# A two-layer network on one core: expert tiles split into gate, up and down parts, softplus placed earlier, a table of its own for the gather

## The reference, cut to what matters

```
x  = x + L0_attn(layernorm(x)) + L0_ffn(layernorm(x))
x  = x + L1_attn(layernorm(x)) + L1_ffn(layernorm(x))
```

## Time and profile before

| | |
|---|---|
| profiled execution | 2730.79 us |
| its span (first to last instruction) | 2729.0 us |
| median of three runs | 2729.32 us |
| busy: PE, DVE, ACT, POOL | 2148.3, 1660.9, 1149.4, 935.1 us |
| mean granted TensorE clock | 0.874 of full |
| DMA | 175.06 MB, mean 64 GB/s |

### The profile page before, as it was taken

One profiled execution on the slowest core, in us unless ns is written; L12 is line 12 of the kernel. 1 busy time (PEld: TensorE's weight loads), 2 busy tenths in 40 slices (PEclk: granted clock), 3 DMA queues, 4 the chain that ended last, 5 costly groups with the idle time before them and its releaser, 6 DMA issues.

```text
span 2729.0 us, 38765 instructions
## 1 busy us (share of the span) xinstructions
PE 2148.3 (79%) x11640; PEld 1493.1 (55%) x11640; DVE 1660.9 (61%) x2929; ACT 1149.4 (42%) x2667; POOL 935.1 (34%) x581
## 2 busy tenths in 40 slices
PE   3257788887888788887788787887788878888985
PEld 1033456565665556555566555665566555565664
DVE  2954876458754786447765577656774478654432
ACT  2212464235633465234552355424563346523641
POOL 0320482017610384005630077202751048401601
PEclk9568789888899898987898898998889989899997
DMA  2000012211212111220112211221122211132223
GB/s 94 0 16 1 26 52 80 76 68 41 80 58 101 45 48 60 82 97 34 58 56 91 76 41 54 89 88 49 47 70 71 98 41 46 64 119 70 72 93 115
DMA packets 82452, 175.06 MB, mean 64 GB/s; under 512 B 11448, under 2 KB 42560, under 8 KB 81984
## 3 DMA queue, kind: packets, MB, share of 16 engines
q1 hardware_dynamic: 78144, 164.05, 17.7%
q0 software_dynamic: 4096, 8.40, 1.0%
HBM read 123.71 MB, written 15.14 MB: 51 GB/s over the span
## 4 chain that ended last, share of the span: by engine, by line
PE 46%; DVE 16%; issue 15%; POOL 13%; ACT 6%; DMA 3%; SPq 1%; POOLq 0%; DVEq 0%; ACTq 0%
PE G L921 9%; PE G L1043 5%; POOL Y L1935 4%; PE G L1028 3%; DVE HS L1521 3%; POOL REG L1946 3%; POOL REG L1949 2%; POOL YG L1960 2%; PE FM L733 2%; PE G L1060 2%; PE G L932 2%; PE FM L1017 2%; PE FM L891 2%; PE FC L1005 2%; DVE SL L1686 1%
## 5 line engine op out<-in xcount | busy, mean ns | idle before, releaser
L1043 PEld LDWEIGHTS G<-REG 128*128 128x128 f32 x2560 | 361.9, 205 | 64.9 <-issue 51.0
L1521 DVE TENSOR_TENSOR_SCAN HS<-DA,D 128x1024 f32<-128x1024 f32 x128 | 362.7, 2833 | 20.2 <-ACT DA L1204 19.6
L1043 PE MATMUL G<-REG 128*128 128x64 f32 x2560 | 368.9, 278 | 3.2 <-DVE REG L1825 3.2
L1935 POOL TENSOR_TENSOR Y<-Y,HC 128x1024 f32<-128x1024 f32 x114 | 278.4, 2442 | 214.4 <-DVE HC L1543 214.0
L1028 PE MATMUL G<-ident,REG 128*128 128x128 f32 x1280 | 248.8, 295 | 121.2 <-ACT REG L1324 119.2
L921 PEld LDWEIGHTS G<-XGT,MW 128*128 128x128 f32 x1920 | 290.0, 235 | 53.9 <-issue 53.9
L921 PE MATMUL G<-XGT,MW 128*128 128x128 f32 x1920 | 297.4, 321 | 19.0 <-DMA MW<-moe 19.0
L1324 ACT ACTIVATE REG<-G 128x128 f32<-128x128 f32 (+3 forms) x512 | 223.0, 435 | 158.3 <-PE G L1028 154.1
L1946 POOL TENSOR_TENSOR REG<-REG,cos_t 128x512 f32<-128x512 f32 x128 | 178.4, 1394 | 297.0 <-ACT REG L1300 292.1
L1028 PEld LDWEIGHTS G<-ident,REG 128*128 128x128 f32 x1280 | 154.7, 154 | 168.4 <-issue 145.7
L1273 ACT ACTIVATE SL<-G 128x512 f32<-128x512 f32 x120 | 71.6, 597 | 411.5 <-PE G L921 411.5
(11 more groups left out here) (285 smaller groups left out, 3921.2 us busy)
## 6 DMA issues: line engine op xcount, KB each, us to landing
MW<-moe SPq DMA_DIRECT2D x120, 768.0 KB, 4.2
REG<-ROT SPq DMA_DIRECT2D x256, 128.0 KB
EW<-experts SPq DMA_DIRECT2D x16, 514.5 KB, 4.0
XG<-x_rows SPq DMA_DIRECT2D x8, 960.0 KB, 5.5
y_rows<-YO SPq DMA_DIRECT2D x120, 64.0 KB, 1.5
X<-xT SPq DMA_DIRECT2D x8, 256.0 KB, 5.9
W<-weights SPq DMA_DIRECT2D x1, 2048.0 KB, 9.5
REG<-xT SPq DMA_DIRECT2D x8, 256.0 KB, 2.7
```

The costliest lines, as they stand in the source:

```text
L1043: mm = pe.matmul(G[3][:, col:col + DK], PT[:, n % 2, c * P:(c + 1) * P], V[:, c, j * P + h * DK:j * P + (h + 1) * DK], start=c == 0, stop= ...
L1521: dve.tensor_tensor_scan(HS[:, :, :].rearrange("p h s -> p (h s)"), DA[:, n % 2, :, :].rearrange("p h s -> p (h s)"), D1[:, :, :].rearrang ...
L1935: pool.tensor_tensor(Y[:, :, :], Y[:, :, :], HC_EARLY if early else HC[:, n % 2, :, :], ALU.add).then_inc(y_add.sem, 1)
```

## The change

- A tile's `token_use` becomes three parts. `gate` is its four gate products with a semaphore of their own (`gg_mm`), `up` the four up products, `down` the down product. PARTS_AFTER deals the 45 parts over the steps, no more than two after any step; the last, the down product of tile 14, follows step 28 within the list. ACT runs the Tanh with the gate part, waiting for `gg_mm`; DVE runs both products with the up part.
- Softplus (pieces 11 and 12 of the front) moves from after steps 21 and 22 to after steps 17 and 18.
- The gather reads a table of its own, `place_kept`, written from the same places at step 19 of phase 2. The cast into `place_i` at step 9 no longer waits for the picks' sum.

```diff
-        X_AFTER = {0: (1,), 1: (2,), 2: (3,), 3: (4,), 4: (5, 6), 6: (7,), 7: (8,), 10: (9,), 11: (10,), 21: (11,), 22: (12,)}
-        weight = [0.5 if 18 <= p <= 21 else 1.1 for p in range(F_STEPS)]
-        def t_share(p):
-            return 1 + round(sum(weight[:p]) / sum(weight) * (MOE_TILES - 1))
+        X_AFTER = {0: (1,), 1: (2,), 2: (3,), 3: (4,), 4: (5, 6), 6: (7,), 7: (8,), 10: (9,), 11: (10,), 17: (11,), 18: (12,)}
+        TOKEN_PARTS = [("gate", 0), ("up", 0)]
+        for i_ in range(1, MOE_TILES):
+            TOKEN_PARTS += [("gate", i_), ("up", i_), ("down", i_ - 1)]
+        TOKEN_PARTS.append(("down", MOE_TILES - 1))
+        PARTS_AFTER = (0,1,2,1,2,1,2,1,2,1,2,1,2,2,2,1,2,1,2,1,1,1,1,2,2,1,2,1,2,1)
...
-        PHASE_1 = [("o", 0), ("x", 0), ("t", 0), ("f", -1)]
+        PHASE_1 = [("o", 0), ("x", 0), ("t", TOKEN_PARTS[0]), ("t", TOKEN_PARTS[1]), ("f", -1)]
+        PHASE_1 += [("t", u) for u in TOKEN_PARTS[2:2 + PARTS_AFTER[0]]]
+        part_ = 2 + PARTS_AFTER[0]
         for p in range(F_STEPS):
             PHASE_1.append(("f", p))
-            PHASE_1 += [("t", u) for u in range(t_share(p), t_share(p + 1))]
+            PHASE_1 += [("t", u) for u in TOKEN_PARTS[part_:part_ + PARTS_AFTER[p + 1]]]
+            part_ += PARTS_AFTER[p + 1]
...
 (PE)
-            def up_gate(b, i):
+            def gate_rows(b, i):
                 if i >= 2:
                     pe.wait_ge(hh_d.sem, hh_d.at(b, i - 1))
                 pe.wait_ge(xt_copy.sem, xt_copy.at(b, i // TILES + 1))
                 pe.wait_ge(mw_in[i % SLOTS].sem, mw_in[i % SLOTS].at(b, i // SLOTS + 1))
-                g = 2 * (i % 2)
-                for half in range(2):
-                    for c in range(CHUNKS):
-                        at = half * HID + c * P
-                        mm = pe.matmul(G[g + half][:, c * P:(c + 1) * P], MW[:, i % SLOTS, at:at + P], XGT[:, i, :], start=True, stop=True)
+                for c in range(CHUNKS):
+                    mm = pe.matmul(G[2 * (i % 2)][:, c * P:(c + 1) * P], MW[:, i % SLOTS, c * P:(c + 1) * P], XGT[:, i, :], start=True, stop=True)
+                mm.then_inc(gg_mm.sem, 1)
+            def up(b, i):
+                for c in range(CHUNKS):
+                    at = HID + c * P
+                    mm = pe.matmul(G[2 * (i % 2) + 1][:, c * P:(c + 1) * P], MW[:, i % SLOTS, at:at + P], XGT[:, i, :], start=True, stop=True)
                 mm.then_inc(ug_mm.sem, 1)
...
 (ACT)
-                act.wait_ge(ug_mm.sem, ug_mm.at(b, i + 1))
+                if part == "down":
+                    rows_done(b, i)
+                if part != "gate":
+                    return
+                act.wait_ge(gg_mm.sem, gg_mm.at(b, i + 1))
...
 (DVE)
+                if part != "up":
+                    return
...
+                dve.wait_ge(ug_mm.sem, ug_mm.at(b, i + 1))
                 dve.wait_ge(sx_d.sem, sx_d.at(b, i + 1))
...
             def number_places(b):
-                dve.wait_ge(ys_d.sem, ys_d.at(b - 1))
                 dve.wait_ge(xg_in.sem, xg_in.at(b - 1))
                 dve.wait_ge(place_d.sem, place_d.at(b, 11))
                 dve.tensor_copy(place_i[:, :, :].rearrange("p k t -> p (k t)"), places[:, 56:64]).then_inc(place_d.sem, 1)
+            def keep_places(b):
+                dve.wait_ge(ys_d.sem, ys_d.at(b - 1))
+                dve.tensor_copy(place_kept[:, :, :].rearrange("p k t -> p (k t)"), places[:, 56:64]).then_inc(kept_d.sem, 1)
...
+                    if s == KEEP_AT:
+                        keep_places(b)
...
 (POOL, gather)
-                    pool.wait_ge(place_d.sem, place_d.at(t))
+                    pool.wait_ge(kept_d.sem, kept_d.at(t))
...
-                                        in_offset=bass.IndirectOffsetOnAxis(ap=place_i[:, k, c:c + 1], axis=0)).then_inc(yg_in.sem, 16)
+                                        in_offset=bass.IndirectOffsetOnAxis(ap=place_kept[:, k, c:c + 1], axis=0)).then_inc(yg_in.sem, 16)
```

More of the change, by code:

```diff
@@ L162, in build @@
         place_i = sb("place_i", [P, PICKS, TILES], U32)
+        place_kept = sb("place_kept", [P, PICKS, TILES], U32)
         tile_i = sb("tile_i", [1, 16], I32)
@@ L340, in build @@
         place_d = signal("place_d", 12)
+        kept_d = signal("kept_d")
         xw_d = signal("xw_d", PICKS)
@@ L348, in build @@
         xt_mm, xt_copy = signal("xt_mm", TURNS), signal("xt_copy", TURNS)
+        gg_mm = signal("gg_mm", MOE_TILES)
         ug_mm = signal("ug_mm", MOE_TILES)
@@ L376, in build @@
                  d1_mm, d2_mm, lg_mm, wb_mm, e1_mm, e2_mm, v_mm, pj_mm, sc_mm, pt_mm, pv_mm, ot_mm, wo_mm, gl_mm,
-                 xtok_mm, rank_mm, xt_mm, ug_mm, dn_mm, yt_mm] + [n.by_pe for n in norms]
+                 xtok_mm, rank_mm, xt_mm, gg_mm, ug_mm, dn_mm, yt_mm] + [n.by_pe for n in norms]
         by_act = [biased, u_silu, r_silu, soft, da_exp, qsq_d, ksq_d, q_gelu, g_act, d1_gelu, rt_act,
@@ L381, in build @@
                   gk_d, lni_d, hsm_d, m1_d, h2_d, m2_d, l0a_d, xm_d, rt_d, wb_d, yf_d, l0f_d, x2_d, xn2_d, rot_d,
-                  nm_d, rec_d, o_d, x3_d, gt_d, pick_d, place_d, sx_d, hh_d, out_d] + [n.by_dve for n in norms]
+                  nm_d, rec_d, o_d, x3_d, gt_d, pick_d, place_d, kept_d, sx_d, hh_d, out_d] + [n.by_dve for n in norms]
         by_pool = [du_d, skip_y, y_add, y_gate, xnb_d, rope_d, xw_d, ys_d]
@@ L902, in turn_rows, with token_use @@
                 mm.then_inc(xt_mm.sem, 1)
[L904 to L908, removed]
-            def up_gate(b, i):
+            def token_use(b, part, i, following):
+                if part == "gate":
+                    gate_rows(b, i)
+                elif part == "up":
+                    up(b, i)
+                else:
+                    down(b, i)
+            def gate_rows(b, i):
                 if i >= 2:
@@ L1077, in phase_1 @@
                 each_step(b, t, f, filter_step, token_use, front_start, attention_end, early_scan)
-                if t is not None:
-                    down(t, MOE_TILES - 1)
             def phase_2(b, f, t):
@@ L1266, in rows_done, with token_use @@
                 act.activation(YO[:, i % SLOTS, :], G[4][:, 0:D], ACT.Copy).then_inc(yo_copy.sem, 1)
-            def token_use(b, i, following):
-                act.wait_ge(ug_mm.sem, ug_mm.at(b, i + 1))
+            def token_use(b, part, i, following):
+                if part == "down":
[3 more added lines that the diff above has]
+                act.wait_ge(gg_mm.sem, gg_mm.at(b, i + 1))
                 if i >= 2:
@@ L1341, in phase_1 @@
                 each_step(b, t, f, filter_step, token_use, front_start, lambda t, b: None, early_scan)
-                if t is not None:
-                    rows_done(t, MOE_TILES - 1)
             def phase_2(b, f, t):
```

7 lines of the change are left out of this document (3 added, 4 removed).

## The result

The changed kernel took 2618.7 us (median of four runs, 2604.7 to 2623.97), the kernel before 2729.26 beside it: a ratio of 0.958, 95% interval 0.951 to 0.965. The forecast was 2638, its range 2590 to 2692. The profiled execution took 2623.97 us with a span of 2622.1, against 2729.0 before: 106.9 us less.

A forecast was written before the change was run, and what follows sets the result against it. PE is the busiest engine of both phases, yet idle about 26 us of each first phase. Terms 30 + 1 + 54 + 5 + 0 + 1 = 91 us off 2730.8 give 2639.8, as median 2638 us; range 2590 to 2692.

The forecast's parts named there:

- Thirds, idle time: First phase: tiles in thirds fill PE's gaps, idle time from 25.8 to 18.1 us, 7.7 less per lap.
- Clock: First phase: with a third less PE idle time, 0.01 of granted clock comes back, 1.2 us per lap.
- clock comes back: Rival: PE granted 0.95 instead of 0.87 to 0.91 in first phases, about 15 us per lap, time 2598; chance 0.17.
- Own table: Second phase: DVE's cast no longer waits for POOL, 5 us per lap in six laps, 30 us; bounds 2.7 and 6.6.
- the shift at XN2: End of first phase: second phase's first matmul starts about 0.9 us after XN2 instead of 6.57; part of the 7.7.
- Softplus: First phase: 2.4 us gone after the gelus, some 3 of ACT's 7.2 left among them; net 0, bounds -3 and +3 per lap.
- Lap without front and last stage: Outside the six full laps: 5 us without a following front, 1 for the last lap's wait, 1 in the last stage.
- Signs of failure that were named: First phase: PE idle time stays at 26 us, DVE waits for the up third, or a tile's weights come late.
- latency: Rival: the first phase is a chain through PE, ACT and DVE; thirds give 2 us per lap, time 2685; chance 0.18.
- tables: Rival: ACT's 7.2 us of table loads and passes among the gelus uncovered, 23 us slower, time 2752; chance 0.03.

The follow-up runs named there:

- f1: The changed kernel once more, unaltered, on a second chip: 2592.0 us, ratio 0.947 to the kernel before.
- e2: The kernel before with the tiles in thirds alone, no own table, softplus after steps 21 and 22: 2656.2 us, ratio 0.974.
- e4: The changed kernel with softplus back after steps 21 and 22: 2603.3 us, ratio 0.951 to the kernel before.
- e1: The kernel before with the gather's own table alone: 2685.8 us, ratio 0.985.
- g3: The changed kernel with gate, up and down parts put behind one another at one step, signals kept: 2679.3 us, ratio 0.978 to the kernel before.
- h1: The changed kernel with parts dealt finely up to step 18 and put together from there: 2601.3 us, ratio 0.952 to the kernel before.
- e3: The kernel before with softplus alone moved to after steps 17 and 18: 2714.6 us, ratio 0.994.

## Why the prediction was right, and where it was not

- **Total and sign**: 91 us forecast, 106.9 measured between the two profiled executions. This is the sum of first phases that gave 41 us more than their term, second phases that gave 30 less, and 5 more in the rest. That the total came out this near is luck in part, for the two errors have opposite signs. And the 15.9 us a lap of the first phase lie above the 12 with which the range's lower end was added up, though the prediction's own bound was 17.
- **Thirds, idle time**: 7.7 a lap forecast, 10.4 measured (26.0 to 15.6). The closed gaps are among those named: root chain, squares (2.3 left before the variance, where the prediction wanted none), and XN2, which was 0.71 for a forecast 0.9.
- **Clock**: the mis-sized term. 1.2 us a lap was assumed, one hundredth of clock; the mean clock rose by four, from 0.88 to 0.92, and the busy time of the same matmuls fell by 5.4. The price of a hundredth was right, its number not. In the first phase the rival "clock comes back" was nearer than the forecast: it wanted 0.95 and 15 us, and the phase reached 15.9 at about 0.92, as idle time fell more too. f1, at 0.92 to 0.97, shows that both happen.
- **Own table**: that the wait and its 2.12 us cast would go was right; the copy cost 2.6 us in five laps of eight and 0.16 in three, 1.7 on the mean for a forecast 1.1. The term of 5 a lap was too small: 7.7 alone and 6.0 beside the thirds. The stretch from one reciprocal to the next did fall to the 21 us that the prediction named, 21.0 on the mean, but that agreement is luck: it is 19.1 or 19.2 in four laps and 24.0 and 25.8 in two, f1 has 25.3, and alone the table gave 1.2 us there.
- **The step that failed**: the shift at XN2, "that I count in full". The first matmul did move 5.6 us closer to XN2, and the first phase shows it in full: of its 15.9 us, 10.2 lie before XN2 starts and 5.6 behind. But the end of the second phase did not move with it: its length grew by 5.3 a lap without the table (e2) and by 7.0 with it (e4 against e1), where the prediction had nothing for the thirds' effect on that phase. This is why the second phase, cut at the first matmul, gained nothing although the table gave its 6 us. In g3 and h1 some 3 us of the shift are kept. What takes back the shift was not isolated; that it is the order in which VectorE and GpSimd meet is a guess from the rows above.
- **Softplus**: net 0 within -3 and +3. Alone -2.4, beside the thirds nothing that can be told. The four loads among the gelus are in e3 as well, and there the move still gained. ACT_TABLE_LOADs rose from 42 to 56, the 14 foreseen: those of the earlier trace rows are gone, and the experts' gelus have their own (group of instructions, count, busy us, mean ns, idle before):

```profile
L1259 ACT ACT_TABLE_LOAD x14 | 18.0, 1283 | 0.3
```

The experts' matmuls wait 2.8 us for gelus in a middle lap, inside the 1 to 3.
- **Lap without front and last stage**: 5 + 1 + 1 forecast, 7.2 + 1.2 + 2.2 measured.
- **Signs of failure that were named**: idle time did fall; VectorE waits for the up part by 22.7 us over the laps, no longer than 3.1 at once, and the first phase gained all the same; weights come late by 2 us a lap, so the concern was real and small.
- **Rivals**: latency (2685) and tables (2752) are excluded by the interval, and by g3 for the first: what the fine dealing fills is worth 13 us a lap. The total lies about midway between the forecast, 2638, and the clock rival, 2598, and f1's 2592 is nearer to the rival.

## What to carry to other kernels

Work dealt in pieces of the size of the gaps gained twice: less idle time, and a higher granted clock on the same matmuls. But measure the phase after it too, and cut it at the instruction that releases it: here an earlier first matmul looked like 5.6 us gained in one phase and was given back in the next. Where VectorE's scans and GpSimd's sums take turns all the time, the stretch around a removed wait is a poor measure of what it was worth: compare whole phases, every lap of them, and two parts of a change each with and without the other.

## What the runs showed of the hardware

- A 128x8 cast takes 0.16 us or 2.59, two 128x32 products 0.28 or 3.35, a 128x1024 scan 2.28 or up to 5.22, and GpSimd's sum of 128x1024 2.36 or up to 4.44, by which of the two engines is held. Two laps that lay within 0.8 us of one another up to such a meeting took 162.6 and 172.8 us; that the rest follows from it wasn't tested by itself.
- The executions of one program spread from 2571 to 2624 us; its second phases within one execution from 161.8 to 179.6.
- A transfer of 128 KB issued 0.7 us behind one of 960 KB on the same queue made its readers wait 4.1 us; with the large one issued later, no swap of a full lap was waited for over 1.1.
